# ScalarE's adapter rounding ahead of its last step for the scored rows, an early exponential, and a later first side load

## The reference

```
W = w_cond[cond_ids]                              # 64 x 64 for each sample
y = einsum('bct,bcd->bdt', x, W)
x = x + y @ W_base.T + b_base + (routed low-rank part of y, top 2 of 8 experts, rank 16)

w = w1[adapter_ids]                               # 1024 x 1024 for each sample, ids 3 to 7
z = einsum('bsi,boi->bso', x, w)
scores = 8 * softmax(z @ Wr.T + br)               # over 8 heads
x = x + 2 * einsum('bshr,hor,bsh->bso', z @ A.T, B, scores)
```

## Time and profile before

| | us |
|---|---|
| median of 3 runs | 763.69 (763.29 to 764.03) |
| profiled execution, its own time | 764.91 |
| its span | 763.1 |
| PE busy | 738.4 (97%) |
| DVE busy | 397.5 (52%) |
| POOL busy | 251.0 (33%) |
| ACT busy | 202.7 (27%) |

### The profile page before, as it was taken

One profiled execution on the slowest core, in us unless ns is written; L12 is line 12 of the kernel. 1 busy time (PEld: TensorE's weight loads), 2 busy tenths in 40 slices (PEclk: granted clock), 3 DMA queues, 4 the chain that ended last, 5 costly groups with the idle time before them and its releaser, 6 DMA issues.

```text
span 763.1 us, 14239 instructions
## 1 busy us (share of the span) xinstructions
PE 738.4 (97%) x4768; PEld 720.1 (94%) x4768; DVE 397.5 (52%) x1201; ACT 202.7 (27%) x490; POOL 251.0 (33%) x150
## 2 busy tenths in 40 slices
PE   5999999999999999999999999999999999999993
PEld 5899999999999999999999999999999999999982
DVE  2532035566555555555555665555555555556652
ACT  1211122333222323322223332223233232233220
POOL 1110143333333333333333333333333333333321
PEclk9999999999999999999999999999999999999996
DMA  8999301010111111111110101111111111101001
GB/s 288 403 404 363 142 1 52 33 56 30 55 55 55 55 55 55 55 55 55 55 53 31 54 29 54 55 55 55 55 55 55 55 55 55 52 32 55 6 36 42
DMA packets 16679, 62.18 MB, mean 81 GB/s; under 512 B 2068, under 2 KB 2068, under 8 KB 16660
## 3 DMA queue, kind: packets, MB, share of 16 engines
q1 hardware_dynamic: 15122, 55.09, 19.4%
q0 software_dynamic: 1232, 6.33, 2.2%
q10 hardware_dynamic: 306, 0.53, 0.2%
HBM read 45.16 MB, written 16.78 MB: 81 GB/s over the span
## 4 chain that ended last, share of the span: by engine, by line
PE 95%; DMA 2%; POOLq 1%; DVE 0%; SPq 0%; ACT 0%; issue 0%; POOL 0%; ACTq 0%; DVEq 0%
PE main_ps L285 20%; PE main_ps L286 20%; PE main_ps L287 20%; PE main_ps L400 9%; PE turn_ps L298 8%; PE low_ps L344 4%; PE turn_ps L344 4%; PE turn_ps L332 4%; PE out_ps L285 2%; DMA stage<-in_w 2%; PE out_ps L286 2%; PE out_ps L287 2%; POOLq L52 1%; PE low_ps L387 0%; PE out_ps L381 0%
## 5 line engine op out<-in xcount | busy, mean ns | idle before, releaser
L285 PE MATMUL main_ps<-w_lo,yT 128*128 128x386 f32 (+1 forms) x768 | 271.3, 353 | 0.0
L286 PE MATMUL main_ps<-w_hi,yT 128*128 128x386 f32 (+1 forms) x768 | 260.4, 339 | 0.0
L287 PE MATMUL main_ps<-w_hi,yT 128*128 128x386 f32 (+1 forms) x768 | 260.2, 339 | 0.0
L808 POOL TENSOR_TENSOR adapter<-folded,adapter 128x1088 fp32r<-128x1088 f32 x64 | 160.5, 2529 | 18.7 <-issue 18.7
L285 PEld LDWEIGHTS main_ps<-w_lo,yT 128*128 128x128 f32 x768 | 145.2, 189 | 0.1
L286 PEld LDWEIGHTS main_ps<-w_hi,yT 128*128 128x128 f32 x768 | 145.2, 189 | 0.0
L287 PEld LDWEIGHTS main_ps<-w_hi,yT 128*128 128x128 f32 x768 | 144.6, 188 | 0.0
L804 POOL TENSOR_TENSOR wait_col<-zero_cols 128x1 f32<-128x1 f32 x32 | 6.2, 193 | 367.9 <-ACT adapter L464 367.9
L622 DVE COPY hg<-main_ps 128x136 f32<-128x136 f32 x32 | 9.6, 300 | 165.2 <-PE main_ps L287 165.2
L797 POOL TENSOR_TENSOR ring<-ring,bias_rows 128x1024 f32<-128x1024 f32 x32 | 76.3, 2383 | 48.7 <-PE turn_ps L298 41.7
L400 PE MATMUL main_ps<-ag_raw,stage 128*128 128x136 f32 x640 | 77.3, 285 | 11.2 <-DMA stage<-in_w 11.2
(11 more groups left out here) (96 smaller groups left out, 775.6 us busy)
## 6 DMA issues: line engine op xcount, KB each, us to landing
stage<-in_w SPq DMA_DIRECT2D x40, 512.0 KB, 8.3
ring<-in_x SPq DMA_DIRECT2D x32, 512.0 KB, 3.3
out<-ring SPq DMA_DIRECT2D x32, 512.0 KB, 2.6
y<-in_w POOLq DMA_DIRECT2D x5, 464.0 KB, 6.9
bias_rows<-in_w POOLq DMA_DIRECT2D x5, 464.0 KB, 6.5
ag_raw<-in_ag SPq DMA_DIRECT2D x1, 544.0 KB, 3.8
cond_table<-in_w_cond ACTq DMA_DIRECT2D x2, 256.0 KB
y<-in_b POOLq DMA_DIRECT2D x1, 512.0 KB, 6.8
```

Source lines behind the costliest of these rows:

```text
L285: pe.matmul(dst, st_hi, mv_lo, start=start, stop=False, skip_group_check=True)
L286: pe.matmul(dst, st_lo, mv_hi, start=False, stop=False, skip_group_check=True)
L287: return pe.matmul(dst, st_hi, mv_hi, start=False, stop=stop, skip_group_check=True)
L808: pool.tensor_tensor(adapter[:, :, b, 1, :], folded[:, bass.ds(e, 1), :, :].rearrange("p a k n -> p (a k) n"), adapter[:, :, b, 0, :], ALU ...
```

## The change

Three edits. ScalarE's `adapter_high(r)` moves ahead of `lwT_high(r-1)`, behind `score_exps(r-1)`. ScalarE computes one exponential of the identity's first 8 columns into `exp1` (overwritten later) before it reads the first adapter's id. GpSimd's first side load waits for the third piece of the first adapter, not for the first.

```diff
                 if l1:
                     score_exps(q, r - 1)
+                if l0:
+                    adapter_high(q, r, adapters)
                 if l1:
                     lwT_high(q, r - 1)
-                if l0:
-                    adapter_high(q, r, adapters)
...
+            act.wait_ge(const_set, 6)
+            act.activation(exp1[:, :], identity[:, 0:EXPERTS], ACT.Exp)
             e = first_adapter(act)
...
-            pool.wait_ge(unit_landed[0], 16)
+            pool.wait_ge(unit_landed[2], 16)
             load_side(0)
             load_side(1)
```

## The result

The changed kernel took 760.41 us (median of 6 runs, 758.78 to 760.80) against 763.94 for the kernel before, run beside it (6 runs, 763.29 to 764.84): 3.5 us less by the medians. The ratio of the runs is 0.9944, 95% interval 0.9932 to 0.9955, which is 3.4 to 5.2 us with 4.3 in the middle. The forecast was 759.3, that is 4.4 us less, with a range of 757.2 to 761.5. Sign and range hold. By the medians the forecast time was 1.1 us too low and the gain 0.9 too large; by the ratio the gain is as forecast.

What follows compares the result with a forecast made beforehand. TensorE, busy 738.4 of 763.1 us, was taken as the bound. Start 1.1, second edit 0, loop 0, tail 2.1 and clock 1.2 sum to 4.4 us: from the median of 763.69 to 759.3, range 757.2 to 761.5.

Steps and rivals of the forecast that it cites:

- The start: TensorE's pause at the first adapter's fifth piece: it lands at 20.2, 1.1 us earlier, with 0 and 1.9 kept as bounds.
- My first step: At the start, from 13.4 to 15.9, the table's and SP's queues alone move 0.74 MB, 0.37 each.
- The loop: In the 30 iterations, L495 starts up to 0.2 us late, hidden with 0.4 us to spare: 0 us.
- The tail: Last tile: GpSimd's subtractions end earlier, so make_low can start at 745.05 in place of 747.18: 2.1 us gained.
- The clock: make_low in the tail, after a pause of 2.3 us: full clock gains 2.0, a fall 0 to 1.5; 1.2 us taken.
- Rival 1: Start gives nothing, since the fifth piece lands when all three queues' bytes have passed: 760.4 us, chance 0.22.
- my third bound: At the start, nothing is gained in rate and all the same bytes pass before the fifth piece: gain 0.
- Rival 2: Full gains: the start's pause goes (1.9) and the clock stays up through make_low (2.0): 757.7 us, chance 0.25.
- Rival 3: In the tail another wait takes the place of the old one, leaving only 1.1 at the start: 762.6 us, chance 0.06.
- rival 4: In the loop, setting the copies' addresses makes L495 1.2 us late in 30 iterations: slower, 777 us, chance 0.04.
- my signs of being wrong: L285 waiting for VectorE's L708 in the loop, a first piece's landing moving by itself, or the fifth landing at 21.3 again.

## Why the prediction was nearly right

**The start, 1.1 forecast.** 1.2 by the run of that edit alone, 1.1 by the two profiled executions counted from the first piece, some 1.4 by the means of all traces. The size holds, and the assumption under it (the table brings the low rate: 267 GB/s) holds too, but the way from one to the other did not, and the agreement is in good part luck. I said that the fifth piece would land at 20.2, 10.9 us after the first, and still hold TensorE; it landed 9.8 after the first, held nobody, and the pause went to the sixth piece. My first step was right: in the 2.5 us from 12.25 on (the place of my 13.4) the table moved 0.37 MB and SP's queue 0.35. Then two terms were off. GpSimd's data began at 16.0, 7.9 us after the first piece where I had put 6.6, 5.1 after the issue and not 3.9, and until then SP's queue had only the table beside it. And SP had 0.83 MB to move up to the fifth piece, not 1.0. I never asked what the piece behind the fifth would do. By my own numbers it would have come 0.52 / 0.195 = 2.7 us after 20.2, at 22.9, where TensorE took it up at 23.2 before (21.32 and 1.85): a gain of 0.3 and not 1.1. The early fifth piece and the forgotten sixth cancelled.

**The second edit, 0 forecast.** 0 measured. The first copy starts at 12.21, as soon as its piece is done, and nobody had waited for it.

**The loop, 0 forecast.** The period stayed at 20.55. L495 was not late at all: 0.04 behind the transpose's end, before and after.

**The tail, 2.1 forecast.** 2.10 (4.43 less 2.33) by the traces, and with the clock out of the account the two kernels' difference is the sum of both ends.

**The clock, 1.2 forecast: this is the term that was mis-sized.** It gave 0.5 us in the profiled execution, 0.8 by the means of make_low over three traces with the old pause and four with the new, and 0.6 to 0.8 by the two kernels with added products. I had set 2.0 us and 0 as the ends and taken the middle, as if the length of the pause decided. It does not alone: after 2.33 us of pause make_low ran wholly at full clock in one trace (the 2.0 that I allowed for) and took 3.2, 3.2 and 3.5 us in three. Nor did I count the last output products, which ran at half clock before and after, since a second pause of 3.2 us lies ahead of them which the change doesn't touch. The too large clock term is some 0.5 us of the 0.9 by which the gain was missed at the medians; the remainder is inside the interval, and by the ratio there is nothing left to explain.

**The rivals.** Rival 1 (nothing at the start) falls with the run of that edit, 0.6 to 2.1 us. But its picture, that the same bytes only change places, fits the sixth piece's landing; what was wrong in it, and in my third bound, is that reordering gives 0. Rival 2 would have needed both ends in full. Rival 3's form (subtractions slower beside VectorE's additions) did not come, and the reason that I gave was thin: the additions to x1T have one input in SBUF, the other in PSUM. The pair that matters is `lw` and the subtraction, and in the changed kernel only ScalarE's two copies keep them apart, by 2.0 us (in the iteration shown `lw` ends at 408.9 and GpSimd starts at 410.9). Moved one place further it would have been the loss that rival 4 spoke of, by another mechanism. Rival 4's addresses cost nothing that can be seen. And one of my signs of being wrong did come, a first piece's landing that moves by itself: by 1.15 us between the two profiled executions, which is why the start is counted from it here.

## What to carry to other kernels

When a wait goes, work out the next arrival as well as the one that ended it; the pause moves to the next piece in line, and reordering transfers can pay even when no byte moves faster. A pause of TensorE in a tail costs more than its length, since what follows may run at half clock: products nobody reads were worth 2.7 us here, about as much as both steps of the transfer order. What the clock costs behind a pause takes several traces to say. And before work on GpSimd is moved earlier, look at which VectorE instructions with two inputs in SBUF it will now meet, and who starts first; if it is a matter of 0.03 us, put a wait between them.

## What the runs showed of the hardware that I had not expected

- VectorE's product of two SBUF tensors, 0.29 us, took 2.6 us when GpSimd's subtraction had begun 0.03 us before, and 0.29 when it began 0.04 after; so in all 31 tiles of that trace. A GpSimd fill held a VectorE instruction on 8 columns for 0.5 us.
- The table's two loads (64 partitions each, from one source) took the whole core from some 413 to 262 to 267 GB/s while they lasted, in a queue of their own or not.
- The landing of the very first piece differs by 1.6 us between profiled executions (7.7 to 9.3) with nothing changed ahead of it.
- After a pause of 2.33 us the clock fell within make_low in three traces, in the changed kernel's 0.6 us after TensorE had begun again, and stayed full through it in a fourth.
